# Loading each row of packed sums in two requests, one for each half of the partitions

## The chip, the cores and the metric

The kernel runs on one core of a Trainium2 chip. The metric is device time in microseconds (us) of one execution. Engines are named as in the profile: PE is TensorE (PEld its weight loads), DVE VectorE, ACT ScalarE, POOL GpSimd, SP SyncE, and SPq the queue in which SyncE issues DMA requests. Sixteen DMA engines serve the core.

## The reference

One block of an adaptive-layernorm network for 4 sequences of 512 tokens and 256 channels: a state-space mixer with 32 heads (state size 64, head size 8), then a gated FFN with 1024 hidden channels and a Hadamard transform.

```python
h = layernorm(x) * (1 + ca) + sa
proj = h @ W_in.T
xBC, z, A_log = split(proj)
xBC = causal_conv(xBC, conv_w, taps=4) + conv_b
x_, Bm, Cm = split(xBC)
a  = -softplus(A_log).transpose(0, 2, 1)          # b, head, l
Lm = exp(segsum(a))                               # lower triangle of exp(S[l] - S[s])
M  = einsum('blhn,bshn,bhls->bhls', Cm, Bm, Lm)
y  = einsum('bhls,bshp->blhp', M, x_) + D * x_
x  = x + ga * (y * silu(z + z_bias)) @ W_out.T
h  = layernorm(x) * (1 + cb) + sb
x  = x + gb * (fwht(silu(h @ W1.T) * (h @ W3.T)) @ W2.T)
```

The decay matrix `Lm` is what matters here. With running sums S of softplus along the sequence, an entry is exp(S[s] - S[l]): one factor varies along the partitions, the other along the free dimension and must be the same on all partitions of a half.

## The kernel before

The heads are worked in 8 groups (g) of 4 heads (j), and each group in 4 batches (b), 32 steps n = 4g + b in all. A sequence is cut in 4 chunks of 128 tokens, and inside a chunk the two halves of 64 tokens are packed so that the lower triangle fills less room. Loops over g are hardware loops for groups 1 to 3, 4, 5 and 6; group 0 and the last are written out, with other work woven in.

A step is a pipeline over three batches. TensorE (`step` in the tensor block) projects B and C for step n (four tiles, 24 matmuls of 512 columns, lines 370 to 372), and for the two steps before it makes the states (L565), the scores (L546), the transposes of B (L527), the state products (`inter`, L582) and the products of mixed scores and x (`intra`, L596). ScalarE takes the first tap of each tile's convolution out of PSUM (`last_tap`, L830), computes the decays (`decays`, L864: four exponentials for each head), and moves small results (`b_evacuate`, `state_copies`, `y_evacuate`). VectorE adds the other three taps of each tile (`tap`, L1173, 12 a step) and multiplies scores by decays (`mix_pair`, L1161, 2 a step). GpSimd adds a mask to the loaded sums (`mask`, L1474, 4 a step), scales x (`scale_by_decays`, L1447; `own_x`, L1467) and splits weights into high and low parts (`split_tile`, L1395; `split_ffn`; `butterfly_half`), all in a written order between the masks.

The running sums are computed once, stored to the DRAM tensor `packed_sums` as 256 rows of 384 floats (two rows for each batch and head, one for each half of the partitions), and loaded again by `load_sum` (lines 227 to 233), one request for each step and head: partitions 0 to 63 of `sums[:, j]` get the first row, partitions 64 to 127 the second, each repeated 64 times. The slot `sums[:, j]` has one buffer, so the load for step n and head j waits until the exponentials of step n - 1 and head j are done (`exp_done`). It is issued by SyncE, whose `step` issues in this order: loads for heads 0, 1 and 2, the two stores of y (`store_y`, L240, one for each half of the partitions), the load for head 3, and once in a group the next weights (`load_group`, L291). Each head has a semaphore of its own, `ld_sum0` to `ld_sum3`. Only `mask` waits for it (line 1472); the exponentials wait for the mask, the mix for the exponentials, and `intra` for the mix.

Before the last group SyncE also issues the loads of the tail: `load_rows` (4 requests), `load_y` (8 for each half of the channels, line 182), and gate rows broadcast to all partitions (`gate_loads`, L247). At the start, behind the first four loads of sums, stand swaps of x between halves (L270) and the stores of x (`store_x`, L214), for which ScalarE's taps of step 1 wait because they use the same tile.

```python
for b in range(B):
    step(g, b, (g - 1 if b < 2 else g))
    if b == 1:
        load_group(g + 1)
```

Of the kernel before, what the change touches and what calls it, by code (L numbers as in the profile page):

```python
# [20 lines left out]
NH, HD, NS = 32, 8, 64  # L21
# [5 lines left out]
JH = 4  # L27
# [6 lines left out]
PL = CH // 2 * PW  # L34
# [16 lines left out]
def adaln_ssm_ffn_kernel(nc, u, w_bc, w_x, w_a, w_z, conv, d_rows, z_bias, w_out, w13, w2, c_t, wmod,  # L51
                         consts, out, e_d, gates_d):
    with ExitStack() as ctx:
        def sb(name, shape, dt, where=ctx):
            return where.enter_context(nc.sbuf_tensor(name, shape, dt))

        def sem(name):
            return ctx.enter_context(nc.semaphore(name))
# [47 lines left out]
        sums = sb("sums", [P, JH, L], F32, reg_b)  # L106
# [52 lines left out]
        sums_d = nc.dram_tensor("packed_sums", (B * NH * 2, PL), F32).ap()  # L159
# [14 lines left out]
        s = {n: sem(n) for n in names}  # L174
# [5 lines left out]
        def _(sp):  # L180
# [46 lines left out]
            def load_sum(g, b, j, first=False):  # L227

                q = g * B + b
                if not first:  # L230
                    sp.wait_ge(s["exp_done"], 4 * q + j - 3)
                rows = sums_d[bass.ds((b * NH + g * JH + j) * 2, 2), :].unsqueeze(1)
                sp.dma_start(sums[:, j, 0:PL], rows.to_broadcast([2, NS, PL])).then_inc(s[f"ld_sum{j}"], 16)  # L233

            def store_y(g, b):

# [13 lines left out]
            def step(g, b, gr, last=False):  # L250

                for j in range(3):
                    load_sum(g, b, j)
                if last:
                    sp.wait_ge(s["proj2"], NG * B)
                    load(u2[:], u_b[0], "ld_res")
                    gate_loads()
                if gr is not None:
                    store_y(gr, (b - 2) % B)
                elif b:  # L260
                    sp.wait_ge(s["gate_ev"], 1)
                    sp.dma_start(gates_d, xn[0:B, 0, 0:2, :].rearrange("b k d -> b (k d)")).then_inc(s["st_gates"], 16)
                load_sum(g, b, 3)
# [29 lines left out]
            for j in range(JH):  # L293
                load_sum(0, 0, j, first=True)
# [1064 lines left out]
        def _(pool):  # L1359
            gp = nc.gpsimd  # L1360

            def await_unit(name, value):

                pool.wait_ge(s[name], value)
                pool.sem_inc(s["pool_waits"], 1)
# [11 lines left out]
            for h in range(2):  # L1377
                rows = slice(NS * h, NS * (h + 1))
# [89 lines left out]

            def mask(n, j):

                await_unit(f"ld_sum{j}", 16 * (n + 1))
                v = sums[:, j, 0:PL].rearrange("p (k l) -> p k l", k=2)[:, :, 0:P].rearrange("p k (e l) -> p k e l", e=2)
                far = far_above[:].unsqueeze(1).unsqueeze(1).to_broadcast([P, 2, 2, NS])
                gp.tensor_tensor(v, v, far, ALU.add).then_inc(s["masked"], 1)  # L1474
# [21 lines left out]
            def front_step(g, b):  # L1496

                n = g * B + b
                own_x(g, n, b, False)
                y_add(0, 0)  # L1500
                mask(n, 0)
                y_scale(0, 1)
                y_add(0, 1)
                mask(n, 1)
                mask(n, 2)
                scale_by_decays(g, n, b, False)
                mask(n, 3)
# [147 lines left out]
```

## Time and profile before

| | |
|---|---|
| median of 3 runs | 793.7 us (793.3 to 793.97) |
| profiled execution | 792.76 us |
| its span, first to last instruction | 791.0 us |
| mean granted TensorE clock in the span | 0.86 of 2.4 GHz |
| DMA | 46,879 packets, 59.36 MB, mean 75 GB/s |

Of the DMA packets, 40,948 are under 2 KB; one row of packed sums is 1,536 bytes. A row of the page's group list gives line, engine, operation, output and inputs, count, busy time, the mean of one in ns, and the idle time of the engine just before them with what ended most of it. A row of a timeline gives start and length in us, engine, line, operation, count, and in brackets the idle time before and its releaser; several instructions of one kind in a row are merged. The share of DMA is that of all 16 engines: 1.00 would be all of them busy.

### The profile page before, as it was taken

Reading aid. Unit: us, or ns where it says so; the run is one execution under the profiler, and the core shown is the slowest. Engines: PE = TensorE matmul, PEld = TensorE weight load, DVE = VectorE, ACT = ScalarE, POOL = GpSimd, SP = SyncE. Lnnn points to the kernel's source line nnn. Section 1 sums busy time; section 2 is a strip of 40 time slices with the busy share of each in tenths; the row PEclk is TensorE's granted clock in tenths of the full one; section 3 lists DMA queues with packets and bytes.
Section 4 is the critical chain, followed back from the end, with each engine's and each line's share of the span. In section 5 each row is a group of like instructions: output and inputs, shape, how many; then the busy total and the mean of one; then the engine's idle time right before and its main releaser. Section 6 shows DMA issues by size and latency. Waiting matters only on the chain.

```text
span 791.0 us, 18982 instructions
## 1 busy us (share of the span) xinstructions
PE 583.9 (74%) x7091; PEld 465.1 (59%) x7092; DVE 456.7 (58%) x746; ACT 378.3 (48%) x988; POOL 238.9 (30%) x465
## 2 busy tenths in 40 slices
PE   8967567749656774956577497647555799999998
PEld 4745445637444553744355375535444589898987
DVE  7966556545556664544566554463564556575743
ACT  3756455445545644545565454553545433232331
POOL 5712253343235234334524442241234100000000
PEclk9997978779877886989697788869786899999999
DMA  7442111211211121312112111214114531230000
GB/s 256 189 135 81 55 55 55 78 56 56 76 53 53 53 76 59 99 54 76 54 54 76 53 60 53 76 53 114 53 54 138 136 111 54 73 88 27 1 27 27
DMA packets 46879, 59.36 MB, mean 75 GB/s; under 512 B 4212, under 2 KB 40948, under 8 KB 46584
## 3 DMA queue, kind: packets, MB, share of 16 engines
q1 hardware_dynamic: 46840, 58.87, 23.5%
q8 instruction: 21, 0.34, 0.2%
q14 instruction: 18, 0.15, 0.1%
HBM read 48.75 MB, written 9.05 MB: 73 GB/s over the span
## 4 chain that ended last, share of the span: by engine, by line
DMA 51%; PE 24%; SPq 10%; ACT 4%; POOL 4%; issue 3%; DVE 2%; ACTq 0%; POOLq 0%; DVEq 0%
DMA sums<-packed_sums 48%; PE ps L370 7%; PE ps L372 7%; PE ps L371 7%; SPq L233 4%; ACT decay L864 3%; SPq L240 3%; SPq L182 2%; POOL sums L1474 2%; PE ps L663 1%; DMA x_channels<-acc 1%; DVE acc L1085 1%; DMA y_parts<-yt_sb 1%; POOL wg_lo L1395 1%; SPq L270 1%
## 5 line engine op out<-in xcount | busy, mean ns | idle before, releaser
L1173 DVE SCALAR_TENSOR_TENSOR acc<-ps,cw_dve,acc 128x511 f32<-128x511 f32 (+2 forms) x384 | 258.2, 741 | 183.5 <-ACT acc L830 183.4
L864 ACT ACTIVATE decay<-sums,p_slot 128x128 f32<-128x128 f32 (+1 forms) x512 | 149.7, 364 | 219.1 <-POOL sums L1474 209.9
L1474 POOL TENSOR_TENSOR sums<-sums,far_above 128x256 f32<-128x256 f32 x128 | 93.4, 730 | 365.6 <-DMA sums<-packed_sums 355.7
L370 PE MATMUL ps<-ht_hi,wg_hi 128*128 128x512 f32 x256 | 120.4, 470 | 39.4 <-POOL wg_lo L1395 39.4
L527 PE MATMUL ps<-cst,acc 128*128 128x128 f32 x192 | 43.0, 344 | 136.5 <-ACT b_tok L854 135.1
L371 PE MATMUL ps<-ht_lo,wg_hi 128*128 128x512 f32 x256 | 112.0, 437 | 0.0
L372 PE MATMUL ps<-ht_hi,wg_lo 128*128 128x512 f32 x256 | 111.6, 436 | 0.0
L527 PEld LDWEIGHTS ps<-cst,acc 128*128 128x128 f32 x192 | 24.6, 167 | 144.2 <-ACT b_tok L854 129.8
L830 ACT ACTIVATE acc<-ps,cw_act 128x512 f32<-128x512 f32 x128 | 92.8, 772 | 20.3 <-DMA x_channels<-acc 12.4
L1161 DVE TENSOR_TENSOR mix<-ps,decay 128x768 f32<-128x768 f32 x64 | 60.9, 952 | 59.0 <-PE ps L546 46.3
L370 PEld LDWEIGHTS ps<-ht_hi,wg_hi 128*128 128x128 f32 x256 | 54.7, 214 | 54.9 <-POOL wg_lo L1395 45.1
L546 PE MATMUL ps<-acc 64*64 64x128 f32 (+1 forms) x2048 | 62.5, 264 | 1.9 <-DVE mix L1161 1.9
L372 PEld LDWEIGHTS ps<-ht_hi,wg_lo 128*128 128x128 f32 x256 | 54.8, 214 | 14.1
L371 PEld LDWEIGHTS ps<-ht_lo,wg_hi 128*128 128x128 f32 x256 | 55.3, 216 | 9.6
L546 PEld LDWEIGHTS ps<-acc 64*64 64x64 f32 x2048 | 53.3, 144 | 7.8 <-issue 3.8
L999 ACT ACTIVATE silu_sb<-ps 128x512 f32<-128x512 f32 x32 | 19.1, 598 | 78.7 <-PE ps L372 78.7
L370 PE MATMUL ps<-h_hi,w_hi 128*128 128x512 f32 x128 | 50.5, 394 | 0.0
L372 PE MATMUL ps<-h_hi,w_lo 128*128 128x512 f32 x128 | 49.9, 390 | 0.0
L371 PE MATMUL ps<-h_lo,w_hi 128*128 128x512 f32 x128 | 49.9, 390 | 0.0
L1312 DVE TENSOR_TENSOR hid<-ps,silu_sb 128x512 f32<-128x512 f32 x32 | 22.1, 691 | 41.4 <-ACT silu_sb L999 41.3
L1400 POOL TENSOR_TENSOR rstd<-vareps,minus_half 128x4 f32<-128x4 f32 x8 | 8.4, 1047 | 119.9 <-DVE vareps L1055 117.4
L370 PE MATMUL ps<-w_hi,hid_hi 128*128 128x256 f32 x128 | 36.9, 289 | 0.2 <-DVE stage L1328 0.2
(143 smaller groups left out, 926.3 us busy)
## 6 DMA issues: line engine op xcount, KB each, us to landing
sums<-packed_sums SPq DMA_DIRECT2D x128, 192.0 KB
wg_raw<-in_w_bc SPq DMA_DIRECT2D x8, 512.0 KB, 12.0
y_parts<-yt_sb SPq DMA_DIRECT2D x64, 64.0 KB, 6.8
stage<-y_parts SPq DMA_DIRECT2D x64, 64.0 KB
u_sb<-in_u SPq DMA_DIRECT2D x4, 512.0 KB, 4.4
stage<-in_w SPq DMA_DIRECT2D x1, 2048.0 KB, 13.4
x_channels<-acc SPq DMA_DIRECT2D x8, 256.0 KB, 2.5
ee<-running_sums SPq DMA_DIRECT2D x8, 256.0 KB, 4.2
```

The costliest lines, as they stand in the source:

```text
L233: sp.dma_start(sums[:, j, 0:PL], rows.to_broadcast([2, NS, PL])).then_inc(s[f"ld_sum{j}"], 16)
L240: sp.dma_start(rows, yt_sb[NS * h:NS * (h + 1), b % 2, :]).then_inc(s[f"st_y{b % 2}"], 16)
L370: mm(o, w_hi, x_hi, start=first, stop=False)
L371: mm(o, w_hi, x_lo, start=False, stop=False)
L372: return mm(o, w_lo, x_hi, start=False, stop=last)
L527: i = nc.tensor.transpose(ps[:, 6, c * P:(c + 1) * P], acc[:, b % 2, p, c * P:(c + 1) * P], ident)
L546: i = mm(ps[NS * at:NS * (at + 1), 2 + a, o:o + P - NS * h], acc[own, b % 2, p, c * P + NS * h:c * P + NS * (h + 1)], acc[own, b % 2, 2 + ...
L830: af(acc[:, b % 2, t, :], ps[:, PROJ_BANK[t], :], ACT.Identity, bias=cw_act[:, t, 1:2], scale=cw_act[:, t, 0:1]).then_inc(s[f"tap_a{t}"], 1)
L864: i = af(decay[:, j, own], sums[:, j, own], ACT.Exp, scale=-1.0, bias=p_slot[:, b * CH + n, j:j + 1])
L1161: tt(mix[:, 2 * p:2 * p + 2, 0:PL], ps[:, 2:4, 0:PL], decay[:, 2 * p:2 * p + 2, 0:PL], ALU.mult).then_inc(s["mixed"], 1)
L1173: stt(a[:, d:], ps[:, PROJ_BANK[t], 0:L - d], cw_dve[:, t, TAPS - 1 - d:TAPS - d], a[:, d:], ALU.mult, ALU.add).then_inc(s[f"taps{t}"], 1)
L1474: gp.tensor_tensor(v, v, far, ALU.add).then_inc(s["masked"], 1)
```

## The change

`load_sum` issues two requests in place of one. The first gives one row to partitions 0 to 63, the second the next row to partitions 64 to 127. Both raise the head's semaphore by 16, and `mask` waits for 32 a step in place of 16. Bytes, destination, order of the loads and the wait on `exp_done` stay.

```diff
                 if not first:
                     sp.wait_ge(s["exp_done"], 4 * q + j - 3)
-                rows = sums_d[bass.ds((b * NH + g * JH + j) * 2, 2), :].unsqueeze(1)
-                sp.dma_start(sums[:, j, 0:PL], rows.to_broadcast([2, NS, PL])).then_inc(s[f"ld_sum{j}"], 16)
+                for h in range(2):
+                    row = sums_d[bass.ds((b * NH + g * JH + j) * 2 + h, 1), :]
+                    sp.dma_start(sums[NS * h:NS * (h + 1), j, 0:PL], row.to_broadcast([NS, PL])).then_inc(s[f"ld_sum{j}"], 16)
...
             def mask(n, j):
 
-                await_unit(f"ld_sum{j}", 16 * (n + 1))
+                await_unit(f"ld_sum{j}", 32 * (n + 1))
```

## Rows read from the trace of the kernel before

**Rows 1.** The page: busy time by engine, and the last chain by line.

```profile
PE 583.9 (74%) x7091; PEld 465.1 (59%) x7092; DVE 456.7 (58%) x746; ACT 378.3 (48%) x988; POOL 238.9 (30%) x465
...
DMA sums<-packed_sums 48%; PE ps L370 7%; PE ps L372 7%; PE ps L371 7%; SPq L233 4%; ACT decay L864 3%; SPq L240 3%; SPq L182 2%; POOL sums L1474 2%; PE ps L663 1%; DMA x_channels<-acc 1%; DVE acc L1085 1%; DMA y_parts<-yt_sb 1%; POOL wg_lo L1395 1%; SPq L270 1%
```

**Rows 2.** The waits: who waited for whom, us in total, times, longest.

```profile
POOL sums L1474 <- DMA sums<-packed_sums: 355.7, 119, 9.3
ACT decay L864 <- POOL sums L1474: 209.9, 105, 7.2
```

**Rows 3.** Timeline of POOL, 395 to 430 us: masks of one slot.

```profile
407.52 0.72 POOL L1474 TENSOR_TENSOR sums<-sums,far_above 128x256 f32<-128x256 f32 x1 [3.40 <-DMA sums<-packed_sums]
...
424.40 0.73 POOL L1474 TENSOR_TENSOR sums<-sums,far_above 128x256 f32<-128x256 f32 x1 [3.40 <-DMA sums<-packed_sums]
```

**Rows 4.** Windows of 1 us; last three columns: granted clock, DMA share, GB/s.

```profile
606.00:607.00 1.00, 0.00 (x0) 0.00 (x0) 0.00 (x0) 0.23 (x1) 0.92 (x2) 0.50 1.07 362
...
404.00:405.00 1.00, 1.00 (x6) 0.78 (x5) 0.78 (x1) 0.76 (x3) 0.12 (x1) 1.00 0.41 113
...
400.00:401.00 1.00, 1.00 (x54) 0.58 (x54) 1.00 (x2) 0.98 (x4) 0.00 (x0) 1.00 0.13 48
```

**Rows 5.** DMA issues: count, KB each, median us from issue to landing.

```profile
y_parts<-yt_sb SPq DMA_DIRECT2D x64, 64.0 KB, 6.8
...
x_channels<-acc SPq DMA_DIRECT2D x8, 256.0 KB, 2.5
```

**Rows 6.** SyncE's queue: the first load; then issues by line, ns min/median/max.

```profile
38.87 0.63 SPq L233
...
L233 SPq DMA_DIRECT2D sums<-packed_sums x128: 503/2466/5201, 38.9 to 610.1; - x128
...
L240 SPq DMA_DIRECT2D y_parts<-yt_sb x64: 490/598/5587, 85.5 to 632.9; - x64
```

**Rows 7.** Timeline of PE, 324 to 338 us: scores of two steps.

```profile
325.62 0.90 PE L546 MATMUL ps<-acc 64*64 64x128 f32 x32
...
335.91 0.90 PE L546 MATMUL ps<-acc 64*64 64x128 f32 x32
```

**Rows 8.** Windows: us, busy of PE, PEld, DVE, ACT, POOL, then clock, DMA.

```profile
60.00:600.00 540.00, 359.92 (x5726) 282.41 (x5726) 300.08 (x429) 283.31 (x814) 199.16 (x407) 0.81 0.20 65
...
631.40:791.00 159.60, 155.93 (x880) 136.90 (x876) 91.12 (x179) 50.23 (x85) 3.02 (x3) 1.00 0.18 52
```

**Rows 9.** Timeline, 318 to 332 us: two mixes and one head's exponentials.

```profile
318.70 0.96 DVE L1161 TENSOR_TENSOR mix<-ps,decay 128x768 f32<-128x768 f32 x1 [5.37 <-PE ps L546]
...
328.42 1.17 ACT L864 ACTIVATE decay<-sums,p_slot 128x128 f32<-128x128 f32 x4 [0.56 <-POOL sums L1474]
...
331.77 0.95 DVE L1161 TENSOR_TENSOR mix<-ps,decay 128x768 f32<-128x768 f32 x1
```

**Rows 10.** Timeline, 62 to 64 us: the start of step 1.

```profile
62.95 0.78 ACT L830 ACTIVATE acc<-ps,cw_act 128x512 f32<-128x512 f32 x1 [12.45 <-DMA x_channels<-acc]
...
63.76 0.75 DVE L1173 SCALAR_TENSOR_TENSOR acc<-ps,cw_dve,acc 128x511 f32<-128x511 f32 x1 [9.99 <-ACT acc L830]
```

**Rows 11.** Timeline of SyncE's queue before the last group.

```profile
532.80 0.58 SPq L182 DMA_DIRECT2D ee<-running_sums  x1
...
541.15 4.14 SPq L233 DMA_DIRECT2D sums<-packed_sums  x3
```

**Rows 12.** Timeline of PE and DVE, 587 to 591 us: step 31.

```profile
587.30 0.90 PE L546 MATMUL ps<-acc 64*64 64x128 f32 x32
...
590.42 4.04 DVE L1173 SCALAR_TENSOR_TENSOR acc<-ps,cw_dve,acc 128x511 f32<-128x511 f32 x6 [7.18 <-ACT acc L830]
```

**Rows 13.** The waits from 587.4 to 631.4 us.

```profile
ACT decay L864 <- POOL sums L1474: 19.5, 6, 7.2
```

**Rows 14.** Timeline of PE, and the chain: the same 16 matmuls at two clocks.

```profile
608.46 6.47 PE L663 MATMUL ps<-wo_sb,stage 128*128 128x256 f32 x16 [6.89 <-DVE stage L1201]
...
642.59 3.45 PE ps L663 x16
```

## The prediction

> **What bounds the kernel now.** I read the page first, then the waits, the timeline of GpSimd, the DMA share in short windows, and SyncE's queue. The page [rows 1] shows no engine near its limit: TensorE is busy 74% of the span, VectorE 58%, GpSimd 30%; and the chain that ended last is for 48% of the span the landing of `sums<-packed_sums`, the load that the diff touches. The waits [rows 2] say how this reaches the rest: GpSimd's mask (L1474) waited 355.7 us for that load, 119 times of 128, and ScalarE's exponentials (L864) waited 209.9 us for the mask. In the regular stretch the masks of slot 1 stand at 407.52 and 424.40 us [rows 3]: a step (one head group of one batch, four loads) takes 16.88 us, that is 4.22 us for each load of 192 KB.
>
> Why 4.2 us? The windows [rows 4] answer. Between 400 and 401 us, with loads under way and nothing else, the 16 DMA engines are 0.13 busy and move 48 GB/s. 0.13 of 16 is 2.1 engines. The source of a load is an access pattern whose slowest size is 2 (two rows, each repeated 64 times), and I read the share so: the request is cut in two pieces, each given to one DMA engine, and the other 14 stand idle. 48 GB/s is 24 GB/s for each; 196,608 bytes at 48 GB/s are 4.1 us, and with the stores' share on the same two engines this is the 4.22 us seen. The loop runs at the pace of two DMA engines. Other forms spread: between 404 and 405 us, when the two 64-partition stores of y are moved, the share is 0.41, more than two engines can give; between 606 and 607 us, where one row is broadcast to 128 partitions (L247), it is 1.07 with 362 GB/s.
>
> **The change, part by part.** Each load becomes two requests, with a source of one row repeated 64 times against 64 partitions. Slowest size 64 on both sides, as in the stores of y. So I take each half to run on (about) all 16 engines.
>
> *Landing.* Two halves together carry the same 192 KB. By the 362 GB/s of the other broadcast that is 0.54 us of transfer, by the 24 GB/s of one engine times 16 it is 0.51 us; around it stand the fixed parts. The shortest landings shown are 2.5 us for 256 KB [rows 5], so I take 2.5 us, with bounds 1.8 and, if it stayed as for y's stores now, 6.8 us. Four loads a step then want some 2.1 us of all engines, in place of 16.6 us of two.
>
> *SyncE's queue.* It issues 4 requests more in each step: 8 for sums and 2 for y. Uncongested, an issue is 0.63 us (the first load), at least 0.503; the median of 2.466 and the longest of 5.2 are, as I read it, the queue held up by full engines [rows 6]. y's 64-partition requests cost 0.598 by the median, though they too stand in that queue. 10 x 0.6 = 6.0 us in a step: below what the step will take, so it costs nothing; its cover is that a load is issued when the exponentials have freed its slot and is needed one step later. The slack is a step less 1.17 of exponentials [rows 9], 1.2 of issue, 2.5 of landing and 0.7 of mask, 4.7 us at a 10.3 us step. What is queued behind a waiting load on SyncE is the next load, y's stores and once a group the weights, all with a step or more to spare.
>
> *GpSimd.* The wait value goes from 16 to 32 for a load; no instruction more. Nothing.
>
> *What a step takes when loads are in time.* Between two runs of the same scores, 325.62 and 335.91 us, TensorE works almost without a gap at the full clock of 2.4 GHz [rows 7]: 10.29 us. The other engines' floors come from the window of 60 to 600 us, 31 steps [rows 8]: VectorE 300.1/31 = 9.7, ScalarE 283.3/31 = 9.1, GpSimd 6.4 us. Three engines stand close together; TensorE sets it, at 10.3. To this I add 0.3 for what ScalarE does once in each group of four steps, two casts and three copies; at the 1.17/4 = 0.29 us of one exponential [rows 9] they are 1.5 us, 0.37 a step, most of it on the path: 10.6. Bounds: 10.0, a little above VectorE's floor, and 13.07, the time between two mixes of VectorE at 318.70 and 331.77 [rows 9], a step in which weights and one mask were late.
>
> *The start.* The first load is issued at 38.87. ScalarE waits 12.45 us for the stores of x_channels, and VectorE starts step 1 at 63.76 after 9.99 us idle [rows 10]. These stores stood in SyncE's queue behind loads on the two engines. Free engines end that; the next thing late is VectorE itself, at 63.76 - 9.99 = 53.8 us.
>
> *The last group.* Before it SyncE issues 12 requests for the tail, from 532.80 to 541.15 [rows 11]: 8.35 us of queue against the 4.7 us of slack. The first load behind them will be late by 3.7; with their own 1.5 MB on the engines I take 5 us.
>
> *The tail.* VectorE's taps of step 31 start at 590.42; TensorE has ended that step's state and intra products when it starts the scores at 587.30 [rows 12], and from there I count the tail, to 631.4, where the FFN stretch begins. Of these 44.1 us ScalarE waited 19.5 for masks [rows 13], nearly all on the path; I take off 18, leaving 26. In the FFN, 631.4 to 791.0, TensorE is busy 155.9 of 159.6 us [rows 8], and no `sums` is loaded: unchanged.
>
> *Sum.* Step 1's taps at 53.8; 30 steps x 10.6 = 318.0; 5 for the last group; in a step that flows the taps start before the point from which the tail counts, by 335.91 - (331.77 + 0.95) = 3.2 us [rows 7, 9] (VectorE free, to the scores); tail 26; FFN 159.6. Total 565.6 us of span. The profiled execution took 792.76 us with a span of 791.0, so 1.8 lies around it; and the median of the runs is 793.7, another 0.9. **568 us**, against 793.7: 28% less. As a difference: the steps now take (590.42 - 63.76)/30 = 17.56 us each; 6.96 less in each is 209 us, the start gives 10 and the tail 18, the last group takes 5, and the taps of step 31 move from 3.1 us after the tail's first point to 3.2 before it, which takes 6: 226.
>
> **A rule that speaks against it.** On the requests themselves, row first: 0.13 busy with a request over all 128 partitions, and 0.41 and 1.07 with the two other forms [rows 4]. The Trainium skill, DMA: Bandwidth & Descriptors, section "Rules for kernel authors", says not to bother with two transfers to disjoint partition halves, since both spray across all 16 engines and serialize. By that the time would stay at 793.7. Its premise, that the one transfer sprays over 16, is what the 0.13 denies here. The same page, "Why a DMA increments its semaphore by 16 and not by 1", picks the number of engines as the largest up to 16 that divides the slowest size of both patterns; by it the load has 2 and a half has 16, and the sum is the one above.
>
> **The rivals.**
>
> *The halves don't spread, or serialize on the two engines.* Then 2 x 96 KB take the same 4.1 us, and the time is 793.7, or up to some us more. For it: nothing in the trace shows this very form, one row to 64 partitions from a computed row. Against: the 1.07 of L247 and the 0.41 of y's stores. 3%.
>
> *Slower: the issue price belongs to the form.* Suppose the 2.466 us median is what SyncE pays for a broadcast request. Then a step's queue is 8 x 2.466 + 2 x 0.6 = 20.9 us, and the total 568 + 30 x (20.9 - 10.6) = 877 us. It decides from an issue price of (16.88 - 1.2)/8 = 1.96 us on. Against: the first loads, into empty engines, cost 0.63. 3%.
>
> *TensorE's clock stays as it is.* It was granted 0.81 on average from 60 to 600 us [rows 8], that is 1.2 GHz in 38% of the time, and fell after stretches in which TensorE stood idle. The same 16 matmuls take 3.45 us at 2.4 GHz and 6.47 at 1.2 [rows 14], 1.88 times. If 38% of the time remained slow: 10.3 x (1 + 0.38 x 0.88) = 13.7 us a step, 568 + 30 x 3.1 = 661 us. Against: the idle stretches that came before each fall are the ones that go away. 5%.
>
> *A new wait in the step.* The three engines are so level that order and lateness may keep a step between 11.5 and 13.07: up to 568 + 30 x 2.5 = 643 us. Casts and splits of the weights on GpSimd, which stand between masks, would be the place. 17%.
>
> **How the numbers follow.** The forecast, steps of 10.0 to 11.5, has 72%: 568 - 30 x 0.6 = 550 to 568 + 30 x 0.9 = 595 us, less 2 if the last group's 5 are 3. The range goes on through most of the new-wait case, to a step of 12.8 (634 us): 548 to 635. A measurement tells about 0.2%, 1.6 us, from no change. Faster is everything but the first two rivals: 0.94; same 0.03; slower 0.03.
>
> **What would show it.** Right: in the regular stretch the DMA share no longer sits at 0.13 but stands near 0 with short peaks above 0.5; GpSimd's wait for the load falls from 355.7 to under 60 us; L233's 256 issues have a median of about 0.6 us; masks of one slot are 10 to 11.5 us apart; the granted clock of the steps is near 1; the FFN keeps its 159.6 us. Wrong: a share still at 0.13 (no spread), issues above 2 us (queue), or the clock at 0.8 in the steps.

## The result: 551.4 us, and the profile after

The changed kernel takes 551.44 us (median of 4 runs, 549.59 to 551.84) against 793.61 us of the kernel before beside it: a ratio of 0.6944, 95% interval 0.6928 to 0.6960, 30.6% less. The forecast was 568 us, range 548 to 635. The profiled execution took 551.84 us with a span of 550.1.

The page of the changed kernel: busy time by engine, the granted clock of TensorE in 40 slices, and the chain that ended last by line. Lines below 227 stand one further down than before.

```profile
PE 532.5 (97%) x7091; PEld 430.7 (78%) x7092; DVE 454.7 (83%) x746; ACT 372.4 (68%) x988; POOL 240.2 (44%) x465
...
PEclk9999999999999999999999999899899999999999
...
PE ps L371 18%; PE ps L372 18%; PE ps L373 18%; PE ps L547 8%; PE ps L528 4%; SPq L234 4%; PE ps L597 3%; PE ps L583 3%; PE ps L566 3%; PE ps L664 2%; DMA sums<-packed_sums 1%; DMA gates<-gate_rows 1%; SPq L182 1%; ACT decay L865 1%; ACT acc L831 1%
```

Against [rows 1]: the busy times of VectorE and GpSimd are the same to 1% (454.7 for 456.7, 240.2 for 238.9), TensorE's fell from 583.9 to 532.5 while the granted clock rose from a mean of 0.86 to 0.99. The landing of the sums fell from 48% of the chain to 1%; TensorE's matmuls are now the chain. The kernel went from waiting for a transfer to being bound by TensorE. VectorE is nearly as full: from 241 to 281 us, four steps, TensorE is busy 39.9 us and VectorE 38.9. That TensorE sets the step is read from the chain; no run here shortens the work of one engine alone.

The changed kernel's waits, the issues of the load on SyncE's queue (ns min/median/max), and the issue list (KB each, median us to landing; ... marks rows left out):

```profile
POOL sums L1475 <- DMA sums<-packed_sums: 120.6, 66, 8.5
```

```profile
  ACT decay L865: 1.7, 3
...
L234 SPq DMA_DIRECT2D sums<-packed_sums x256: 465/491/1840, 39.0 to 375.4; - x128
```

```profile
sums<-packed_sums SPq DMA_DIRECT2D x256, 96.0 KB, 2.7
...
y_parts<-yt_sb SPq DMA_DIRECT2D x64, 64.0 KB, 2.0
```

GpSimd still waits 120.6 us for the load, in 66 pieces [rows 2: 355.7]. But ScalarE's exponentials, which waited 209.9 us for the masks before, waited 1.7 us: the wait that is left is idle time of an engine that is early. The stores of y land in 2.0 us in place of 6.8 [rows 5]; as I read it, they had stood behind the loads on the two engines. The kernels below bear this out: the same stores land in 4.7 us beside loads on two engines (`outer2`), 2.7 on four (`outer4`) and 2.0 on eight (`outer8`). The issue's median is 0.491 us for 2.466 [rows 6].

Windows of the changed kernel (last columns: granted clock, DMA share, GB/s) in one step, and the whole FFN stretch:

```profile
257.00:258.00 1.00, 1.00 (x6) 0.82 (x5) 0.71 (x2) 0.97 (x3) 0.43 (x1) 1.00 0.10 37
258.00:259.00 1.00, 1.00 (x6) 0.79 (x5) 1.00 (x2) 1.00 (x4) 1.00 (x2) 1.00 0.66 168
...
390.50:550.10 159.60, 155.91 (x880) 136.88 (x876) 91.77 (x179) 51.11 (x87) 3.02 (x3) 1.00 0.18 53
```

The flat 0.13 of [rows 4] is gone: in these two windows the share is 0.10 and 0.66, and the second is more than two engines can give. Over the four steps from 241 to 281 us its mean is 0.34, with single windows between 0.00 and 0.88. The FFN is the 159.6 us of [rows 8].

The timelines of TensorE and VectorE in the changed kernel: scores of two neighbouring steps, the start of the taps of step 31, the point from which the tail counts, and the first matmul of the tail's end:

```profile
260.56 0.90 PE L547 MATMUL ps<-acc 64*64 64x128 f32 x32
...
270.59 0.90 PE L547 MATMUL ps<-acc 64*64 64x128 f32 x32
...
362.45 4.02 DVE L1174 SCALAR_TENSOR_TENSOR acc<-ps,cw_dve,acc 128x511 f32<-128x511 f32 x6
365.09 0.90 PE L547 MATMUL ps<-acc 64*64 64x128 f32 x32
...
390.47 0.50 PE L371 MATMUL ps<-ht_hi,wz_hi 128*128 128x512 f32 x1
```

A regular step is 10.03 us between these two scores; over 16 steps in the middle, mixes of VectorE at 161.06 and 322.08 us, the mean is 10.06. The sum of the forecast, term by term: the taps of step 1 start at 53.84 (forecast 53.8), the 30 steps up to those of step 31 take 308.6 us (318 + 5), the tail's first point comes 2.6 later (3.2), the tail takes 390.47 - 365.09 = 25.4 (26), the FFN 159.6. Together 550.1 (565.6).

### The profile page after: what moved, and what is told of

The parts are those of the page before. It is cut to its first block, busy times and chain, and to the rows that moved or that the text cites. A ratio compares the mean times of both kernels' runs of the same rounds, so it can differ in the third digit from the quotient of the medians.

```text
span 550.1 us, 19270 instructions
## 1 busy us (share of the span) xinstructions
PE 532.5 (97%) x7091; PEld 430.7 (78%) x7092; DVE 454.7 (83%) x746; ACT 372.4 (68%) x988; POOL 240.2 (44%) x465
## 4 chain that ended last, share of the span: by engine, by line
PE 77%; SPq 7%; DMA 5%; DVE 4%; ACT 2%; issue 2%; POOL 1%; ACTq 0%; POOLq 0%; DVEq 0%
PE ps L371 18%; PE ps L372 18%; PE ps L373 18%; PE ps L547 8%; PE ps L528 4%; SPq L234 4%; PE ps L597 3%; PE ps L583 3%; PE ps L566 3%; PE ps L664 2%; DMA sums<-packed_sums 1%; DMA gates<-gate_rows 1%; SPq L182 1%; ACT decay L865 1%; ACT acc L831 1%
## 5 line engine op out<-in xcount | busy, mean ns | idle before, releaser
L1475 POOL TENSOR_TENSOR sums<-sums,far_above 128x256 f32<-128x256 f32 x128 | 95.2, 747 | 126.6 <-DMA sums<-packed_sums 120.6
L371 PE MATMUL ps<-ht_hi,wg_hi 128*128 128x512 f32 x256 | 107.7, 421 | 2.8 <-POOL wg_lo L1396 2.1
L372 PE MATMUL ps<-ht_lo,wg_hi 128*128 128x512 f32 x256 | 101.7, 397 | 0.0
L373 PE MATMUL ps<-ht_hi,wg_lo 128*128 128x512 f32 x256 | 101.7, 397 | 0.0
L547 PE MATMUL ps<-acc 64*64 64x128 f32 (+1 forms) x2048 | 57.6, 249 | 2.5 <-DVE mix L1162 1.8
L371 PEld LDWEIGHTS ps<-ht_hi,wg_hi 128*128 128x128 f32 x256 | 48.4, 189 | 12.8 <-POOL wg_lo L1396 2.5
L373 PEld LDWEIGHTS ps<-ht_hi,wg_lo 128*128 128x128 f32 x256 | 48.4, 189 | 11.7
L547 PEld LDWEIGHTS ps<-acc 64*64 64x64 f32 x2048 | 48.7, 133 | 8.8 <-issue 3.8
L372 PEld LDWEIGHTS ps<-ht_lo,wg_hi 128*128 128x128 f32 x256 | 48.8, 191 | 8.5
L528 PE MATMUL ps<-cst,acc 128*128 128x128 f32 x192 | 34.9, 290 | 1.8 <-ACT b_tok L855 1.5
L372 PE MATMUL ps<-w_lo,hid_hi 128*128 128x256 f32 x128 | 36.2, 283 | 0.0
```

Of the source, the lines that this page charges most:

```text
L371: mm(o, w_hi, x_hi, start=first, stop=False)
L372: mm(o, w_hi, x_lo, start=False, stop=False)
L373: return mm(o, w_lo, x_hi, start=False, stop=last)
L528: i = nc.tensor.transpose(ps[:, 6, c * P:(c + 1) * P], acc[:, b % 2, p, c * P:(c + 1) * P], ident)
L547: i = mm(ps[NS * at:NS * (at + 1), 2 + a, o:o + P - NS * h], acc[own, b % 2, p, c * P + NS * h:c * P + NS * (h + 1)], acc[own, b % 2, 2 + ...
```

## The experiments

### Which property of the request sets the number of DMA engines

`outer2` and `outer4` keep the two requests of the changed kernel and only write the source's 64 repeats in another way:

```diff
-                    row = sums_d[bass.ds((b * NH + g * JH + j) * 2 + h, 1), :]
-                    sp.dma_start(sums[NS * h:NS * (h + 1), j, 0:PL], row.to_broadcast([NS, PL])).then_inc(s[f"ld_sum{j}"], 16)
+                    row = sums_d[bass.ds((b * NH + g * JH + j) * 2 + h, 1), :].unsqueeze(1)
+                    sp.dma_start(sums[NS * h:NS * (h + 1), j, 0:PL], row.to_broadcast([2, NS // 2, PL])).then_inc(s[f"ld_sum{j}"], 16)
```

> The two halves stay two requests of one row and 64 partitions each, but the source's 64 repeats are written as 2 x 32, so that its slowest size is 2. My theory (the slowest size sets how many DMA engines a request gets): both halves run on two engines, the share of DMA returns to 0.13 in the steps, a load takes 4.2 us again, the step 16.9 us, the time 780 to 800 us. Rival (what helped is that each request has one row and half of the partitions, or that there are two of them): 551 us, unchanged from the changed kernel.

Measured: 796.91 us, 1.0031 times the kernel before (interval 1.0019 to 1.0044). Same bytes, same pieces, same two requests as the changed kernel; one number in the source pattern brings all 242 us back, and 3 more. A window of `outer2` looks as [rows 4]:

```profile
400.00:401.00 1.00, 1.00 (x50) 0.91 (x42) 0.38 (x1) 0.36 (x1) 0.00 (x0) 1.00 0.13 46
```

So it is not the splitting that helped.

The pages also let the engines be counted. The line on DMA packets in the page of the kernel before, of `outer2` and of the changed kernel:

```profile
DMA packets 46879, 59.36 MB, mean 75 GB/s; under 512 B 4212, under 2 KB 40948, under 8 KB 46584
...
DMA packets 47136, 59.37 MB, mean 75 GB/s; under 512 B 4468, under 2 KB 41204, under 8 KB 46840
...
DMA packets 50720, 59.38 MB, mean 108 GB/s; under 512 B 8052, under 2 KB 44788, under 8 KB 50424
```

The pieces of a load are 1,536 bytes, so the packets under 512 bytes are something else. Their number is 3,956 + requests for sums x engines: 128 x 2 in the kernel before, 256 x 2 in `outer2`, 256 x 16 in the changed kernel. With the same 3,956 it comes out to the unit in the kernels below: 4,980 in `outer4` (256 x 4), 6,004 in `outer8` (256 x 8), 4,468 in `columns` (256 x 2), 6,004 in `one_row` (128 x 16), 12,148 in `quarters` (512 x 16) and 4,084 in `no_loads` (8 x 16). What these packets are is not shown; their number goes with the engines of each request.

> As the changed kernel, but the source's 64 repeats are written as 4 x 16: slowest size 4. My theory: four engines at 24 GB/s each move a step's 786 KB in 8.2 us, with y's share 8.4 us, below the 10.03 us that a step takes; so TensorE goes on setting the step and the time is 551 to 570 us (a little more in the last group, where the slack is used up), with landings near 4 us and longer in place of 2.7. Rival (request form alone matters): 551 us with landings unchanged at 2.7 us. Rival (a load must land at once, landing time is on the path): above 600 us.

Measured: 576.51 us (575.38 to 577.63), 6 above the top of my range. The mechanism is as expected: where only loads of sums are moved, the share is 0.27 of 16, 4.3 engines, at 96 GB/s, twice the 48.

```profile
165.00:166.00 1.00, 1.00 (x6) 0.82 (x5) 0.82 (x1) 0.79 (x3) 0.94 (x4) 1.00 0.27 96
```

What I had missed is what a nearly full queue does when anything else comes. Where nothing else comes, the mixes of VectorE are 9.9 to 10.0 us apart as in the changed kernel; where weights or the tail's loads stand between, they are 11 to 13 us apart, and 17.7 once, before the last group. The chain of `outer4` in one of the first groups, at a step of 12.9 us (start us, us, what):

```profile
163.24 5.47 DMA sums<-packed_sums
...
169.56 0.62 POOL w_hi L1548
...
171.66 0.73 POOL wg_lo L1396
...
172.43 0.74 PE ps L371
173.17 0.43 PE ps L372
```

A landing of 5.5 us delays a mask, GpSimd's splits stand in order behind it, and TensorE waits for the weights. The stall costs clock too: the matmuls behind it take 0.43 us where 0.23 is usual, and the mean granted clock from 165 to 175 us is 0.88. Four engines carry the bandwidth of the average step and not the peaks.

`columns` takes the kernel before and makes two requests of each load by columns (`mask` waits for 32 a step, as in the changed kernel):

```diff
-                rows = sums_d[bass.ds((b * NH + g * JH + j) * 2, 2), :].unsqueeze(1)
-                sp.dma_start(sums[:, j, 0:PL], rows.to_broadcast([2, NS, PL])).then_inc(s[f"ld_sum{j}"], 16)
+                for c in range(2):
+                    cols = slice(c * PL // 2, (c + 1) * PL // 2)
+                    rows = sums_d[bass.ds((b * NH + g * JH + j) * 2, 2), cols].unsqueeze(1)
+                    sp.dma_start(sums[:, j, cols], rows.to_broadcast([2, NS, PL // 2])).then_inc(s[f"ld_sum{j}"], 16)
```

> Two requests for each load, but cut by columns: each has two rows, 128 partitions and 192 of the 384 columns, so the slowest size of the source stays 2. My theory: two engines for both, 780 to 800 us if only the bytes count, up to 840 if the shorter pieces of 768 bytes are slower. Rival (more requests in flight give more engines): about 551 us.

Measured: 858.48 us, 8% slower than before. Two requests in flight give no more engines, and pieces of 768 bytes in place of 1,536 cost: neighbouring masks in its trace stand 4.65 us apart where they were 4.14, and in `outer2`, with two requests of whole rows, also 4.14.

```profile
404.00:405.00 1.00, 0.81 (x12) 0.68 (x6) 0.57 (x1) 0.16 (x1) 0.98 (x1) 1.00 0.14 41
```

`one_row` takes the kernel before and makes a single request over all partitions:

```diff
-                rows = sums_d[bass.ds((b * NH + g * JH + j) * 2, 2), :].unsqueeze(1)
-                sp.dma_start(sums[:, j, 0:PL], rows.to_broadcast([2, NS, PL])).then_inc(s[f"ld_sum{j}"], 16)
+                row = sums_d[bass.ds((b * NH + g * JH + j) * 2, 1), :]
+                sp.dma_start(sums[:, j, 0:PL], row.to_broadcast([P, PL])).then_inc(s[f"ld_sum{j}"], 16)
```

> One request for each load over all 128 partitions, with one row for all of them (left out: the upper half's own row; it gets the lower half's). Slowest size 128 on both sides. My theory: all engines, with half of the requests on SyncE: 546 to 552 us, landing about 2.7 us for 192 KB. Rival (one must split in halves to spread): near 790 us. A gain of more than 2 us over the changed kernel would say that the issue of the second half still costs something, most likely in the last group.

Measured: 544.82 us (544.15 to 545.49), landing 3.1 us for 192 KB. Its result is wrong, since the upper half lacks its own row. No split is needed to spread. It is 6.6 us below the changed kernel, more than the 2 us that I had named as the sign that issuing the second half costs something; `no_loads` below asks what.

`outer8`, with `[8, NS // 8, PL]`:

> Halves with the source's 64 repeats written as 8 x 8: slowest size 8, eight engines. A step's loads then take about 4.2 us of these engines, less than half of a step, with 0.7 us more of landing than with 16. 551 to 558 us; if the time is above 565, the number of engines matters by more than their bandwidth.

Measured: 551.16 us (549.61 to 552.71), the changed kernel's time. The series for the same two requests is 796.9, 576.5, 551.2 and 551.4 us for a slowest size of 2, 4, 8 and 64. From 8 on TensorE sets the time and engines buy nothing.

`copies8` goes the other way round: it leaves the request as it was, over 128 partitions with both rows, and stores each row 8 times in the DRAM tensor, so that the source is 16 rows, each repeated 8 times.

```diff
-                rows = sums_d[bass.ds((b * NH + g * JH + j) * 2, 2), :].unsqueeze(1)
-                sp.dma_start(sums[:, j, 0:PL], rows.to_broadcast([2, NS, PL])).then_inc(s[f"ld_sum{j}"], 16)
+                rows = sums_d[bass.ds((b * NH + g * JH + j) * 2 * COPIES, 2 * COPIES), :].unsqueeze(1)
+                sp.dma_start(sums[:, j, 0:PL], rows.to_broadcast([2 * COPIES, NS // COPIES, PL])).then_inc(s[f"ld_sum{j}"], 16)
```

> One request for each load over all 128 partitions with both rows, as in the kernel before, but each row stands 8 times in the DRAM tensor, so that the source is 16 rows, each repeated 8 times: slowest size 16. The price is at the start: 3.1 MB of short pieces stored in 8 requests where 0.4 MB went in 4, before the first load. My theory: the regular step is 10.0 us with a share far above 0.13, although request, bytes, partitions and rows are those of the kernel before; landing near 3 us; the start is 8 to 15 us later; 550 to 563 us. Rival (a request with two different rows in its source, or over both halves, is held to two engines): near 800 us.

Measured: 553.35 us. Regular steps are 10.0 us, and a load lands in 2.8 us:

```profile
sums<-packed_sums SPq DMA_DIRECT2D x128, 192.0 KB, 2.8
```

```profile
160.00:170.00 10.00, 9.99 (x187) 8.08 (x186) 9.73 (x15) 9.22 (x29) 6.92 (x14) 1.00 0.29 92
```

With the destination, the bytes and the two rows of the kernel before in one request, only the slowest size is another, and 240 us are gone. The stores at the start cost what was expected: VectorE's first mix is at 67.83, against 57.79 in the changed kernel. It ends only 2 us behind it, so 8 of the 10 come back later: with half as many requests the slow steps of the last group are 11.9 and 9.6 us and the stretch into the tail 15.2, where the changed kernel has 13.2, 10.9 and 17.1; the two slow steps at the start are 10.1 and 10.7 for its 10.6 and 12.1. (The stores, not shown, write each row through a source repeated 8 times.)

### What the loads still cost

`no_loads` raises the semaphore and issues nothing after the first four loads (the later loads are left out, so its result is wrong; the mask's constant, not shown, is smaller):

```diff
+                if not first:
+                    sp.sem_inc(s[f"ld_sum{j}"], 32)
+                    return
                 for h in range(2):
```

> Left out: all loads of packed sums after the first four (later steps use what the slots hold; SyncE raises the semaphore by 32 where it would issue, after the same wait; the mask's constant is made smaller so that sums stay finite). It asks what the loads still cost. My theory: in a regular step nothing, which stays at 10.0 us because TensorE sets it; only the queue's delays at the start, before the last group and in the tail go, so 540 to 546 us. Rival (landing or masks still pace the regular step): steps below 9.9 us and a time below 535 us.

Measured: 541.08 us (540.74 to 541.42). The regular steps are still 10.0 us: with no load at all a step is not shorter, so neither landing nor bandwidth nor the issue of 8 requests paces it. The whole of what the loads cost in the changed kernel is 10.4 us, and it lies outside the regular steps. Times between every other mix of VectorE show where (read from the timelines): two steps at the start, 10.6 and 12.1 us in the changed kernel, 10.1 and 10.7 in `no_loads`; two of the last group, 13.2 and 10.9 against 10.1 and 9.9; and the one that spans into the tail, 17.1 against 14.7. At each of these places SyncE issues other requests between the loads.

For the start that is not the whole reason. `outer8` issues as many requests in the same order, each dearer (0.611 us), and its two steps there are 10.0 and 10.7, as without loads; a second execution of the changed kernel (`after_again`) has 10.6 and 10.8. In the chain of the changed kernel one issue takes 1.84 us (at 72.17) and one landing 2.88 (at 75.97), and a split of weights and TensorE wait behind them. Why this form is late there and `outer8` is not was not tried.

`quarters` makes four requests of each load, by quarters of the partitions (`for h in range(4)`, row `h // 2`, 32 partitions each, and a wait for 64 a step):

> Four requests for each load, one for each quarter of the partitions, 16 for sums in a step, same bytes. My theory: a further cut buys nothing, and SyncE's queue becomes the bound: back-to-back issues of halves start 0.64 us apart in the changed kernel's trace, so 16 x 0.64 + 1.3 for y = 11.5 us a step against 10.03, and 590 to 600 us in all. Rival (an issue costs the 0.49 us of the median, or less for fewer partitions): 16 x 0.49 + 1.3 = 9.1 us, hidden, 550 to 560 us.

Measured: 567.14 us (566.65 to 567.62). Between what the two theories gave, and 23 us below the range of mine. The price of an issue is lower for this form than for a half, and the regular step stays at 10.0 us. Timeline and issues of SyncE's queue in `quarters`:

```profile
265.42 8.38 SPq L234 DMA_DIRECT2D sums<-packed_sums  x16
...
L234 SPq DMA_DIRECT2D sums<-packed_sums x512: 310/371/1498, 39.9 to 389.6; - x171
```

Sixteen issues pass in 8.38 us, inside the step of 10.0. My 0.64 was the distance of issues in a burst at the start, and 0.491 the median of halves; a request of 32 partitions costs 0.371. The 15.7 us over the changed kernel are nearly all at the three places named above: 13.3 and 15.1 us for the two steps at the start, 14.6 in the last group, 19.4 into the tail, and a first mix 4.4 us later (0.8 of it from before any load of sums); one more step, of 10.9 us, became 12.0. In this kernel a longer queue costs only where it is already the longest.

### A version that beats both

`spread_tail` moves 8 of the 12 requests that stand ahead of the last group behind its first and second step, and the swap of the last batch at the start one step down:

```diff
-            load_y(0, 0)
             for b in range(B - 1):
                 step(NG - 1, b, (NG - 2 if b < 2 else NG - 1))
+                if b < 2:
+                    load_y(0, 0, (b,))
```

> The changed kernel with its 8 requests for y ahead of the last group taken apart: 4 are issued after the first step of that group and 4 after the second, so that no more than four requests stand between two rounds of loads (the four of load_rows stay ahead of it); and the swap of the last batch at the start is issued one step later. My theory (the 3.2 us by which one step of the last group is late come from the queue of 12 requests): that step falls from 13.2 to about 10.5 us, the start gains about 1 us, 546 to 549 us in all. Rival (the last group is late because of the 1.5 MB on the engines, or the delay just moves to the next steps): 550 to 552 us.

Measured: 547.41 us (546.01 to 547.95). The late step falls from 13.2 to 10.3 us and the next from 10.9 to 9.8. SyncE's queue around it in `spread_tail`:

```profile
329.54 3.71 SPq L234 DMA_DIRECT2D sums<-packed_sums  x6
...
336.47 2.62 SPq L182 DMA_DIRECT2D stage<-y_parts  x4
339.14 3.70 SPq L234 DMA_DIRECT2D sums<-packed_sums  x6
```

In the changed kernel the next loads began at 333.78, after 12 requests. That the queue made them late, and not bytes on the engines, is seen in the chain: the landing behind them takes 2.73 us, the median. The lateness costs clock as well. Windows of TensorE in the changed kernel and in `tail_only` (below):

```profile
346.00:347.00 1.00, 1.00 (x3) 0.75 (x3) 1.00 (x3) 0.41 (x2) 0.98 (x3) 0.50 0.46 110
...
346.00:347.00 1.00, 1.00 (x6) 0.77 (x6) 1.00 (x3) 0.97 (x5) 0.00 (x0) 1.00 0.45 145
```

In the changed kernel TensorE stood idle for 1.50 and 0.78 us just before, and the granted clock was 0.50 for the next 3.4 us (1.2 in place of 2.4 GHz); its matmuls took 0.43 us for 0.23. By these numbers some 1.5 us of the late step are clock, an estimate.

The start did not gain in this profile: its first mix was 2.3 us later, 2.2 of it from before any load of sums.

`tail_only` has the move of the 8 requests alone, and the changed kernel ran beside it:

> The changed kernel with only the second of the two moves of spread_tail: the 8 requests for y ahead of the last group go out 4 and 4 after its first two steps. Against the changed kernel run beside it: 3 to 5 us less, 546 to 548 us, with the late step of the last group at 10.3 us in place of 13.2. If it is less than 2 us, the gain of spread_tail was the start's.

> The changed kernel itself, to stand beside tail_only in the same job: 550 to 552 us.

Measured: 547.82 us (547.17 to 549.12) and 551.49 us (550.67 to 552.92), 5 runs each; against the kernel before 0.6904 (0.6890 to 0.6918) and 0.6954 (0.6939 to 0.6969), intervals that don't meet. The move is worth 3.7 us, and the late step is 10.3 us as expected. So `tail_only` is the faster version, by 0.7%.

## Why the prediction was right, point by point

- **What bounds it.** Right. The share of 0.13 was two engines, and the slowest size of the source was the reason: shown by `outer2` and `outer4` (with the split kept), by `copies8` (without a split), and by the counts of packets, which give 2 engines before and 16 after.
- **Landing and bandwidth.** 2.7 us for the 2.5 taken. `no_loads` shows that the value hardly matters as long as it is inside the slack.
- **SyncE's queue.** Right that it hides in a regular step; 0.49 an issue for the 0.6 taken.
- **The step.** This is the term that was mis-sized: 10.6 taken, 10.06 measured as the mean of 16 steps (10.03 between two neighbouring scores). (10.6 - 10.06) x 30 = 16 us is nearly the whole of the 16.6 between forecast and result; the other terms miss by less than 2 us each. Two things were in it. The 10.29 between two scores of the kernel before [rows 7] was read as free of waits, but that step still had a short wait of TensorE for ScalarE, which had waited 0.56 us for a mask [rows 9]. And the 0.3 for once-in-a-group work was counted as on the path; in the changed kernel the steps with it are 10.2 to 10.3 us and their neighbours 9.8 to 10.0.
- **The last group.** 5 taken; the two slow mixes are 13.2 + 10.9 - 20.1 = 4.0 us over. The cause, SyncE's 12 requests, is shown by `spread_tail` and `tail_only`; that some of it is clock was not in the working. That the start would lose too (2.6 us in two steps) stood nowhere in it either.
- **Start, tail, FFN.** 53.84, 25.4 and 159.6 for 53.8, 26 and 159.6.
- **The rule against it.** The advice of the Trainium skill (DMA: Bandwidth & Descriptors, "Rules for kernel authors") against two transfers to disjoint halves holds where the one transfer already spreads, and `one_row` agrees with it: one request over 128 partitions lands in 3.1 us, and its kernel is 6.6 us faster than that with halves. Here the one transfer did not spread. On the number of engines (the Trainium skill, DMA: Bandwidth & Descriptors, "Why a DMA increments its semaphore by 16 and not by 1": the largest number up to 16 that divides the slowest sizes of both patterns), every run here agrees: shares of 0.13 for 2 and 0.27 for 4, and counts of packets that fit 2, 4, 8 and 16 engines.
- **The rivals.** No spread: out. Issue price that belongs to the broadcast form: out, 0.33 to 0.61 us for all forms whose queue was free; the 2.466 was queueing, and it came back as 1.62 in `outer2`. The clock stays at 0.81: out, 0.99 from 60 to 390 us. A new wait in the step: out.
- **The signs.** Mask distance, clock and FFN as written; the issue price is 0.49 for the 0.6. The share left 0.13 and has peaks above 0.5, but it does not stand near 0 between them: its mean is 0.34, 3.4 us of all engines in a step with y and the weights, where the loads alone were put at 2.1. Another was wrong: GpSimd's wait was to fall under 60 us and is 120.6. A busy floor of 6.4 us in a step of 10 leaves about 3.6 us idle, 31 times; the profile puts that to the next thing GpSimd waits for, the load. The sign to watch was ScalarE's wait for the mask.

## What to carry to other kernels

When the share of DMA sits flat at a small multiple of 1/16 while engines wait for loads, look at the slowest size of both access patterns before looking at bytes: a broadcast written as 2 x 64 ran on two engines; each half written as 64 ran on sixteen, and its landing fell from 48% of the chain to 1%. Splitting a request is one way to change that size and not the cheapest: each further request lengthens the issue queue, which cost nothing in the regular loop here and up to 16 us in all (`quarters`), where other requests are already bunched. And after such a change read the wait of the engine that consumes the result, not of the one that receives the transfer.

## What the runs showed of the hardware that was not expected

- The price of an issue on SyncE's queue does not grow with the number of partitions: medians of 0.333 us for one row to 128 partitions, 0.371 for one row to 32, 0.491 for one row to 64, 0.580 for 16 rows x 8, 0.611 for one row written as 8 x 8. It also differs by place in the program: for one row to 64 the median is 0.469 from 100 to 300 us, in the hardware loops, and 0.600 from 65 to 77 us, where the steps are written out. Why was not tried.
- Cutting pieces from 1,536 to 768 bytes on the same two engines raised a load from 4.14 to 4.65 us; two requests of whole rows (`outer2`) left it at 4.14.
- The packets under 512 bytes count the engines of a request: 3,956 + requests x engines, in nine kernels to the unit.
- Loads at 27% of all engines, four of them full, left most steps at 10 us and still cost 25 us in all: the chain of `outer4` holds single landings of 4.3 to 8.5 us.
